# Seven constant products before the first transposes, one weight loaded a place sooner, and x's first two tiles taken singly

## The chip, the cores and the metric

The kernel runs on 1 core of one Trainium2 chip. The metric is the device time of one execution in microseconds (us), inputs and outputs in the chip's memory; lower is better.

## The reference, cut to what matters

For each of 8 graphs with 1024 nodes there are x (1024 x 256) and adj (1024 x 1024, f32, mostly zero). Two layers follow one another; H is the pattern of adj.

```python
H  = (adj != 0);  w = adj[0, :]
Dn = 1 / (H @ w)                    # per node, 0 where the sum is 0
Be = 1 / H.sum(axis=0)              # per column
def conv(x, W, b):
    m = Be[:, None] * (H.T @ (x @ W.T))
    return Dn[:, None] * (H @ m) + b
h  = layer_norm(relu(conv(x, W1, b1)), gamma, beta)
x1 = norm(x + (conv(h, W2, b2) + x))
agg = (adj @ x1) / max(adj.sum(-1), 1e-6)
out = norm(x1 + relu(concat(x1, agg) @ WL.T))
```

## The kernel before

One program works the eight graphs off one after another; `graph(0, ...)` is written out, the others run in a loop. Each engine has its own instruction list, and semaphores tie them together. Nodes are cut into 8 tiles of 128 rows (NT = 8). Every f32 operand of a product with H is split into a high and a low part (`x_hi`, `x_lo`, `m_hi`, `m_lo`), so each product with H is two matmuls.

The stages of a graph on TensorE are S1 (H.T @ x, L1107), S2 (H @ m, transposed, L1183), P and M (times W1: high and low parts, and cross terms, L1211, L1212, L1219), Q (times W2, L1231), S3 and S4 (H.T and H again, L1077), V and VM (times WL) and L (adj @ y, L1077). The next graph's S1 follows.

What concerns the change is the start, up to graph 0's S1. For tile c of adj:

- SyncE's queue (SP) loads the rows, `load_first_rows(c)` (L338), and between them x in pairs of tiles, `load_first_x(j)` (L341), w_row (L357), W1n (L371), W2n (L373) and the rest. SP issues in the order in which these lines stand. ScalarE's own queue loads x's tiles 0 and 1 as one DMA (L527).
- VectorE makes `H[c]` (`build_first_H`, L743), and the low parts of x in pairs (`split_first_x_lo`, L858), then tile c − 2 of the transposed pattern HT (L797), and at some places a row sum of H times w (`sum_Dn`, L758).
- ScalarE makes the high parts of x in pairs (`split_first_x_hi`, L540) and copies the transposed adj out of the banks (`take_adjT`, L571).
- TensorE transposes the tile in two sets of four blocks (`transpose_four`, L1068) and multiplies it into six banks (`s1_step`, L1107), 12 matmuls a tile. In between it transposes the weights: gamma in tile 1, W1 in tile 5, W2 in tile 6, WL in tile 7, each before or between its products, in program order:

```python
for c in range(NT):
    pe.wait_ge(first_rows_loaded[c], 16)
    transpose_adj(c, 0)
    ...
    pe.wait_ge(H_ready, c + 1)
    pe.wait_ge(x_split, c + 1)
    for e in range(N_SIDE):
        if e == 2 and c in BETWEEN:
            transpose_set(BETWEEN[c][0], 0)
        if e == 3 and c > 0:
            transpose_adj(c, 1)
        if e == 5 and len(BETWEEN.get(c, ())) > 1:
            transpose_set(BETWEEN[c][1], 1)
        s1_step(e, c, 0)
```

When six banks are complete, VectorE takes the reciprocals of their column counts (`take_first_rBe`, L840 and L843), ScalarE and VectorE make `m_hi` and `m_lo` (L561, L790), and TensorE works banks 6 and 7. Meanwhile GpSimd adds W2's transposed rows (L441); TensorE's average of them (L1138) uses `mean_n`, a 128 x 128 constant of 1/512. After S1, VectorE does the last row sums, `diagonals` (L890), W1's low and cross parts (L847, L852) and z (L906, L912), GpSimd the cross parts of z (L470), on which M's first product waits.

GpSimd fills the constants first: ident, the ones beside x_hi, eps, zero, mean_n (L417 to L421).

Of the kernel before, what the change touches and what calls it, by code (L numbers as in the profile page):

```python
# [9 lines left out]
ACT = mybir.ActivationFunctionType  # L10

P = 128
# [22 lines left out]
TRANSPOSE_BANKS = (6, 7)  # L35
N_BANKS = 8
Q_FIRST = 5
ROW_BANKS = (0, 1)
ROW_BEHIND = 0
T_SLOTS = 3  # L40
# [8 lines left out]
def graph_net(nc, x, adj, W1, b1, gamma, beta, W2, b2, WL, out):  # L49
    B, C, D = x.shape  # L50
    DH = W1.shape[0]
# [78 lines left out]
    with ctx:  # L130
# [93 lines left out]
        def sem(name):  # L224
            return ctx.enter_context(nc.semaphore(name))
# [4 lines left out]
        raw_loaded = [sem(f"raw_loaded{n}") for n in range(NT // 2)]  # L230
        adjB_loaded = [sem(f"adjB_loaded{n}") for n in range(NT)]
        first_rows_loaded = [sem(f"first_rows_loaded{n}") for n in range(NT)]
        first_x_loaded = [sem(f"first_x_loaded{n}") for n in range(NT // 2)]
        adjT_ready, first_x_hi = (sem(n) for n in ("adjT_ready", "first_x_hi"))
        x_loaded, w_loaded, W2_loaded, W1_loaded, WL_loaded, gamma_loaded, beta_loaded, bias_loaded, table_loaded = (
# [88 lines left out]
        def _(sp):  # L324
# [12 lines left out]
            def load_first_rows(t):  # L337
                sp.dma_start(raw[:, t, :], adj[0, t * P:(t + 1) * P, :]).then_inc(first_rows_loaded[t], 16)  # L338

            def load_first_x(j):  # L340
                sp.dma_start(x_in[:, 2 * j:2 * j + 2, :],  # L341
                             x[0, 2 * j * P:(2 * j + 2) * P, :].rearrange("(t p) d -> p t d", p=P))\
                  .then_inc(first_x_loaded[j], 16)
# [23 lines left out]
            load_first_rows(4)  # L367
            load_first_rows(5)
            load_first_x(3)
            load_first_rows(6)  # L370
            sp.dma_start(W1n[:, :, :], W1.rearrange("(t p) d -> p t d", p=P)).then_inc(W1_loaded, 16)  # L371
            load_first_rows(7)
            sp.dma_start(W2n[:, :, :], W2.rearrange("(t p) d -> p t d", p=P)).then_inc(W2_loaded, 16)  # L373
            sp.dma_start(beta_row[:, :], beta.partition_broadcast(P)).then_inc(beta_loaded, 16)
# [39 lines left out]

        @block.gpsimd
        def _(pool):
            nc.gpsimd.memset(ident[:, :], 0.0).then_inc(ident_zero, 1)  # L417
            nc.gpsimd.memset(x_hi[:, :, D:DP].bitcast(F32), 1.0).then_inc(ones_ready, 1)
            nc.gpsimd.memset(eps_c, NORM_EPS).then_inc(eps_ready, 1)
            nc.gpsimd.memset(zero_c, 0.0).then_inc(zero_ready, 1)  # L420
            nc.gpsimd.memset(mean_n[:, :], 1.0 / DH).then_inc(mean_ready, 1)  # L421
            nc.gpsimd.memset(gW2T[:, :, D:D + 1], 1.0 / DH).then_inc(unit_ready, 1)
            pool.wait_ge(zero_ready, 1)
            pool.wait_ge(ident_zero, 1)
# [99 lines left out]
        @block.scalar  # L524
        def _(act):

            act.dma_start(x_in[:, 0:2, :], x[0, 0:2 * P, :].rearrange("(t p) d -> p t d", p=P))\  # L527
               .then_inc(first_x_loaded[0], 16)
            act.dma_start(gamma_n[0:NH, :], gamma.rearrange("(k p) -> k p", p=P)).then_inc(gamma_loaded, 16)
            act.dma_start(gamma_n[NH:2 * NH, :], b1.rearrange("(k p) -> k p", p=P)).then_inc(gamma_loaded, 16)  # L530
            act.wait_ge(eps_ready, 1)
# [2 lines left out]
            def split_x_hi(b):  # L534
                act.wait_ge(x_loaded, b * IN_B)
                nc.scalar.activation(x_hi[:, :, 0:D], x_in[:, :, :], ACT.Copy).then_inc(x_hi_done, 1)

            def split_first_x_hi(j):
                act.wait_ge(first_x_loaded[j], 16)
                nc.scalar.activation(x_hi[:, 2 * j:2 * j + 2, 0:D], x_in[:, 2 * j:2 * j + 2, :], ACT.Copy)\  # L540
                  .then_inc(first_x_hi, 1)
# [42 lines left out]
                    nc.scalar.activation(gb, set_bank("gamma", 0)[:, 0:2 * NH], ACT.Copy)\  # L584
                      .then_inc(bank_empty[set_of["gamma", 0][0]], 1)

            split_first_x_hi(0)
            for c in range(NT):
                take_adjT(c, 0)
                if c in BETWEEN:  # L590
# [149 lines left out]
        def _(dve):  # L740
# [119 lines left out]

            for c in range(NT):
                build_first_H(c)
                if c % 2 == 0:
                    dve.wait_ge(first_x_hi, c // 2 + 1)
                    split_first_x_lo((c, c + 1))
                if c >= 2:
                    build_HT_columns(c - 2)
                if c in FIRST_DN_AT:
                    sum_Dn(FIRST_DN_AT.index(c), 0, unread, (first_rows_loaded[FIRST_DN_AT.index(c)], 16))
# [188 lines left out]
        def _(pe):  # L1058
            mm = nc.tensor.matmul

            pe.wait_ge(ident_ready, 1)

            def transpose_four(name, part, four):
# [257 lines left out]
```

## Time and profile before

| | |
|---|---|
| median of 3 runs | 1051.92 us (1051.88 to 1051.96) |
| the profiled execution, its own time | 1051.42 us |
| its span | 1049.6 us |
| TensorE, matmuls, busy | 1039.2 us (99%) |
| TensorE, weight loads, busy | 933.2 us (89%) |
| VectorE | 776.7 us (74%) |
| ScalarE | 433.3 us (41%) |
| GpSimd | 435.6 us (41%) |
| memory traffic | 85 GB/s over the span, 353 GB/s from 4.5 to 9.5 us |

The profile is of one execution, and its durations add up to that execution's span. The 1.8 us between its span and its own time lie before and after the instructions. Matmuls are pipelined and their ends are modelled, so the time from the start of one to the start of the next tells the rate. "PEclk" is the clock that the profile says was granted to TensorE, as a share of full speed.

### The profile page before, as it was taken

The numbers are of one execution on the slowest core, as the hardware profiler recorded it, in microseconds if no ns is written. First come the engines' busy times: TensorE is split into PE (matmuls) and PEld (weight loads), VectorE is DVE, ScalarE is ACT, GpSimd is POOL, SyncE is SP. The second block draws the span as 40 slices with busy tenths as digits, with TensorE's granted clock in tenths as the row PEclk, the third lists the DMA queues.
The fourth block names the chain that finished last, engine by engine and source line by source line (L and its number), as shares of the span: only waits on it lengthen the run. The fifth ranks groups of instructions, "written<-read, shape, count | busy, mean of one in ns | idle before, by whom it ended". The sixth has DMA issues, their size and how long they took to land.

```text
span 1049.6 us, 19643 instructions
## 1 busy us (share of the span) xinstructions
PE 1039.2 (99%) x6241; PEld 933.2 (89%) x6241; DVE 776.7 (74%) x1848; ACT 433.3 (41%) x1029; POOL 435.6 (41%) x674
## 2 busy tenths in 40 slices
PE   8999999999999999999999999999999999999997
PEld 8889898898989989899898998989889898888986
DVE  6878786787867878677786778676786777867355
ACT  5553523445234442445325362254622536225350
POOL 0357416434254433534344353543525534265320
PEclk9999999999999999999999999999999999999999
DMA  8065431734227441274414644044440634400001
GB/s 296 3 138 117 98 90 34 152 92 103 64 59 156 96 98 31 60 160 100 90 30 87 133 100 100 20 114 106 100 100 20 142 78 100 110 11 1 2 1 40
DMA packets 72032, 90.01 MB, mean 86 GB/s; under 512 B 15544, under 2 KB 61248, under 8 KB 72000
## 3 DMA queue, kind: packets, MB, share of 16 engines
q1 hardware_dynamic: 63232, 85.49, 35.1%
q10 hardware_dynamic: 8768, 4.10, 1.7%
q8 instruction: 19, 0.31, 0.1%
q14 instruction: 13, 0.11, 0.0%
HBM read 81.14 MB, written 8.42 MB: 85 GB/s over the span
## 4 chain that ended last, share of the span: by engine, by line
PE 99%; DMA 0%; DVE 0%; issue 0%; ACT 0%; DVEq 0%
PE bank L1077 45%; PE bank L1107 12%; PE bank L1183 11%; PE bank L1231 11%; PE bank L1212 3%; PE bank L1219 3%; PE bank L1274 3%; PE bank L1267 3%; PE bank L1268 3%; PE bank L1211 3%; PE bank L1248 1%; PE bank L1068 1%; PE bank L1234 1%; DMA raw<-in_adj_dram 0%; PE bank L1172 0%; DVE xres L779 0%
## 5 line engine op out<-in xcount | busy, mean ns | idle before, releaser
L1077 PE MATMUL bank<-yv,adjT 128*128 128x257 f32 x1024 | 223.3, 379 | 0.0
L1077 PEld LDWEIGHTS bank<-yv,adjT 128*128 128x128 f32 x1024 | 193.6, 189 | 28.7
L566 ACT ACTIVATE small<-mv,small 128x1 f32<-128x1 f32 x192 | 56.0, 291 | 247.8 <-DVE mv L785 144.6
L1077 PE MATMUL bank<-x_hi,H 128*128 128x256 f32 x512 | 125.1, 286 | 0.0
L1231 PE MATMUL bank<-gW2T,hT 128*128 128x257 f32 x512 | 123.7, 385 | 0.0
L1107 PE MATMUL bank<-x_hi,H 128*128 128x258 f32 x512 | 123.6, 289 | 0.0
L1077 PE MATMUL bank<-x_lo,H 128*128 128x256 f32 x512 | 122.4, 280 | 0.0
L1077 PE MATMUL bank<-m_hi,HT 128*128 128x256 f32 x512 | 122.0, 281 | 0.0
L1077 PE MATMUL bank<-m_lo,HT 128*128 128x256 f32 x512 | 121.4, 279 | 0.0
L1107 PE MATMUL bank<-x_lo,H 128*128 128x256 f32 x512 | 119.2, 282 | 0.0
L561 ACT ACTIVATE m_hi<-bank,small 128x256 fp32r<-128x256 f32 x128 | 57.5, 474 | 136.2 <-DVE small L835 75.6
L1231 PEld LDWEIGHTS bank<-gW2T,hT 128*128 128x128 f32 x512 | 93.0, 190 | 11.5
L1183 PE MATMUL bank<-HT,m_lo 128*128 128x512 f32 x256 | 101.8, 398 | 0.0
L1183 PE MATMUL bank<-HT,m_hi 128*128 128x512 f32 x256 | 101.0, 395 | 0.0
L461 POOL TENSOR_TENSOR small<-mv,small 128x1 f32<-128x1 f32 x120 | 30.0, 250 | 170.0 <-DVE small L774 170.0
L1077 PEld LDWEIGHTS bank<-x_hi,H 128*128 128x128 f32 x512 | 96.8, 189 | 0.0
L1077 PEld LDWEIGHTS bank<-x_lo,H 128*128 128x128 f32 x512 | 96.3, 188 | 0.0
L1077 PEld LDWEIGHTS bank<-m_lo,HT 128*128 128x128 f32 x512 | 96.1, 188 | 0.0
L1077 PEld LDWEIGHTS bank<-m_hi,HT 128*128 128x128 f32 x512 | 96.1, 188 | 0.0
L790 DVE SCALAR_TENSOR_TENSOR m_lo<-bank,small,m_hi 128x256 fp32r<-128x256 f32 x128 | 59.2, 481 | 49.3 <-ACT m_hi L561 49.3
L1107 PEld LDWEIGHTS bank<-x_hi,H 128*128 128x128 f32 x512 | 93.9, 190 | 0.5 <-ACT bW_row L607 0.2
L1107 PEld LDWEIGHTS bank<-x_lo,H 128*128 128x128 f32 x512 | 93.1, 190 | 0.2
(132 smaller groups left out, 2203.1 us busy)
## 6 DMA issues: line engine op xcount, KB each, us to landing
raw<-in_adj_dram SPq DMA_DIRECT2D x112, 256.0 KB, 5.8
adjB<-in_adj_dram SPq DMA_DIRECT2D x224, 128.0 KB, 3.1
x_in<-in_x_dram SPq DMA_DIRECT2D x31, 256.0 KB, 6.1
out_dram<-xres SPq DMA_DIRECT2D x108, 64.0 KB, 1.6
raw<-in_adj_dram SPq DMA_DIRECT2D x8, 512.0 KB, 8.8
w_row<-in_adj_dram SPq DMA_DIRECT2D x8, 512.0 KB, 4.7
w_row<-rDn_row ACTq DMA_DIRECT2D x7, 512.0 KB, 9.0
out_dram<-xres SPq DMA_DIRECT2D x4, 256.0 KB, 2.1
```

What stands on the lines that cost most here:

```text
L561: nc.scalar.activation(m_hi[:, e, :], bank(stage, e)[:, 0:D], ACT.Identity, scale=rBe[:, e:e + 1])\
L566: nc.scalar.activation(std[:, i:i + 1], mv[:, which, i, 1:2], ACT.Sqrt, bias=eps_c)\
L790: empties_bank(nc.vector.scalar_tensor_tensor(out=m_lo[:, e, :], in0=bank(stage, e)[:, 0:D], scalar=rBe[:, e:e + 1], in1=m_hi[:, e, :].bit ...
L1077: last = mm(bank(stage, i)[:, 0:n_cols], lhsT, rhs, start=(k == 0 and part == 0), stop=(k == NT - 1 and part == parts - 1))
L1107: last = mm(*args, start=(c == 0 and n == 0), stop=(c == NT - 1 and n == 1))
L1183: last = mm(bank("S2", job)[:, :], m[:, k, d * P:(d + 1) * P], HT[:, k, ch * CH:(ch + 1) * CH], start=(k == 0 and n == 0), stop=(k == NT - ...
L1211: mm(bank("P", j)[:, :], W1_high[:, d, feats], z_high[:, d, nodes], start=(d == 0), stop=False)
L1212: last = mm(bank("P", j)[:, :], W1_low[:, d, feats], z_low[:, d, nodes], start=False, stop=(d == ND - 1))
L1219: last = mm(bank("M", j)[:, :], W1_cross[:, d, feats], z_cross[:, d, nodes], start=(d == 0), stop=(d == ND - 1))
L1231: mm(bank("Q", i)[:, 0:D + 1], hT[:, k, i * P:(i + 1) * P], gW2T[:, k, :], start=(k == 0), stop=(k == NH - 1))
L1267: mm(bank("V", i)[:, :], x1_high[n][:, part], WL_high[:, d, :], start=(d == 0), stop=False)
L1268: last = mm(bank("V", i)[:, :], x1_low[:, n, part], WL_low[:, d, :], start=False, stop=(d == ND - 1))
```

## The change

mean_n is filled first. TensorE, before it waits for ident, multiplies mean_n by itself seven times into bank 7, whose content is not read before it is overwritten. SP issues W1n before adj's tile 6 and no longer behind it. x's tiles 0 and 1 come in two DMAs with a semaphore each, and ScalarE and VectorE split them one at a time: VectorE's list is now H of tile 0, x_lo of tile 0, H of tile 1, x_lo of tile 1.

```diff
+IDLE_PRODUCTS = 7
...
+        first_tiles_loaded = [sem(f"first_tiles_loaded{n}") for n in range(2)]
...
             load_first_x(3)
+            sp.dma_start(W1n[:, :, :], W1.rearrange("(t p) d -> p t d", p=P)).then_inc(W1_loaded, 16)
             load_first_rows(6)
-            sp.dma_start(W1n[:, :, :], W1.rearrange("(t p) d -> p t d", p=P)).then_inc(W1_loaded, 16)
             load_first_rows(7)
...
+            nc.gpsimd.memset(mean_n[:, :], 1.0 / DH).then_inc(mean_ready, 1)
             nc.gpsimd.memset(ident[:, :], 0.0).then_inc(ident_zero, 1)
...
-            nc.gpsimd.memset(mean_n[:, :], 1.0 / DH).then_inc(mean_ready, 1)
...
-            act.dma_start(x_in[:, 0:2, :], x[0, 0:2 * P, :].rearrange("(t p) d -> p t d", p=P))\
-               .then_inc(first_x_loaded[0], 16)
+            for t in range(2):
+                act.dma_start(x_in[:, t, :], x[0, t * P:(t + 1) * P, :]).then_inc(first_tiles_loaded[t], 16)
...
+            def split_first_tile_hi(t):
+                act.wait_ge(first_tiles_loaded[t], 16)
+                nc.scalar.activation(x_hi[:, t, 0:D], x_in[:, t, :], ACT.Copy).then_inc(first_x_hi, 1)
...
-            split_first_x_hi(0)
+            split_first_tile_hi(0)
+            split_first_tile_hi(1)
...
-                if c % 2 == 0:
-                    dve.wait_ge(first_x_hi, c // 2 + 1)
+                if c < 2:
+                    dve.wait_ge(first_x_hi, c + 1)
+                    split_first_x_lo((c,))
+                elif c % 2 == 0:
+                    dve.wait_ge(first_x_hi, c // 2 + 2)
                     split_first_x_lo((c, c + 1))
...
+            pe.wait_ge(mean_ready, 1)
+            for _ in range(IDLE_PRODUCTS):
+                mm(banks[TRANSPOSE_BANKS[1]][:, 0:P], mean_n[:, :], mean_n[:, :], start=True, stop=True)
             pe.wait_ge(ident_ready, 1)
```

TensorE, the start of its list, before (bank is the place of every product; ident and raw are the two operands of a transpose):

```order
L1068 MATMUL bank<-ident,raw 128x128 [waits first_rows_loaded0,ones_ready,ident_ready]
L1068 MATMUL bank<-ident,raw 128x128 x7
L1107 MATMUL bank<-x_hi,H 128x258 [waits bank_empty0,x_split,H_ready]
L1107 MATMUL bank<-x_lo,H 128x256
L1107 MATMUL bank<-x_hi,H 128x258 [waits bank_empty1]
```

TensorE, the same place, now:

```order
L1074 MATMUL bank<-mean_n 128x128 [waits mean_ready]
L1074 MATMUL bank<-mean_n 128x128 x6
L1082 MATMUL bank<-ident,raw 128x128 [waits first_rows_loaded0,ones_ready,ident_ready]
L1082 MATMUL bank<-ident,raw 128x128 x7
L1121 MATMUL bank<-x_hi,H 128x258 [waits bank_empty0,x_split,H_ready]
```

The seven products stand ahead of the first transposes and wait only for mean_n; nothing behind them has changed places.

VectorE, its first tiles, before (H from raw rows, x_lo from x_in and x_hi):

```order
L743 TENSOR_SCALAR H<-raw 128x1024 [waits first_rows_loaded0]
L858 TENSOR_TENSOR x_lo<-x_in,x_hi 128x256 [waits first_x_hi]
L858 TENSOR_TENSOR x_lo<-x_in,x_hi 128x256
L743 TENSOR_SCALAR H<-raw 128x1024 [waits first_rows_loaded1]
L743 TENSOR_SCALAR H<-raw 128x1024 [waits first_rows_loaded2]
```

VectorE, the same place, now (same names):

```order
L750 TENSOR_SCALAR H<-raw 128x1024 [waits first_rows_loaded0]
L865 TENSOR_TENSOR x_lo<-x_in,x_hi 128x256 [waits first_x_hi]
L750 TENSOR_SCALAR H<-raw 128x1024 [waits first_rows_loaded1]
L865 TENSOR_TENSOR x_lo<-x_in,x_hi 128x256 [waits first_x_hi]
L750 TENSOR_SCALAR H<-raw 128x1024 [waits first_rows_loaded2]
```

The second tile's subtraction moved behind H of tile 1; each subtraction waits for its own activation.

## Rows read from the trace of the kernel before

**Rows 1.** The page, chain of waits by engine.

```profile
PE 99%; DMA 0%; DVE 0%; issue 0%; ACT 0%; DVEq 0%
```

**Rows 2.** Timeline of weight loads: start us, us, engine, line, operation [idle before <- releaser].

```profile
4.51 1.57 PEld L1068 LDWEIGHTS bank<-ident,raw 128*128 128x128 f32 x8 [4.51 <-issue]
...
9.49 0.32 PEld L1107 LDWEIGHTS bank<-x_hi,H 128*128 128x128 f32 x1
9.71 0.21 PEld L1107 LDWEIGHTS bank<-x_lo,H 128*128 128x128 f32 x1
9.85 0.19 PEld L1107 LDWEIGHTS bank<-x_hi,H 128*128 128x128 f32 x1
9.97 0.19 PEld L1107 LDWEIGHTS bank<-x_lo,H 128*128 128x128 f32 x1
```

**Rows 3.** Stretch table of PEld: stretch, length, busy (count), granted clock, DMA share, GB/s.

```profile
4.50:9.50 5.00, 4.99 (x25) 1.00 1.05 353
```

**Rows 4.** GpSimd's first fill (timeline), and mean_n's one product (by tile; min/median/max ns).

```profile
0.75 0.20 POOL L417 MEMSET ident<- 128x128 f32 x1 [0.29 <-POOLq L1309]
...
L1138 PE MATMUL bank<-ssum,mean_n x2: 377/377/377, 29.9 to 30.1; 128*128 128x256 f32 x2
```

**Rows 5.** Timeline of ScalarE, the first activation on x.

```profile
4.92 0.63 ACT L540 ACTIVATE x_hi<-x_in 128x512 fp32r<-128x512 f32 x1 [1.23 <-DMA x_in<-in_x_dram]
```

**Rows 6.** Timeline of VectorE: H of tiles 5, 6, 7, HT, reciprocals' start.

```profile
16.77 0.69 DVE L743 TENSOR_SCALAR H<-raw 128x1024 fp32r<-128x1024 f32 x1
...
17.97 0.69 DVE L743 TENSOR_SCALAR H<-raw 128x1024 fp32r<-128x1024 f32 x1
...
20.99 0.69 DVE L743 TENSOR_SCALAR H<-raw 128x1024 fp32r<-128x1024 f32 x1
21.82 0.69 DVE L797 TENSOR_SCALAR HT<-adjT 128x1024 fp32r<-128x1024 f32 x1
...
28.97 0.17 DVE L840 TENSOR_SCALAR small<-bank 128x6 f32<-128x6 f32 x1 [0.75 <-PE bank L1107]
```

**Rows 7.** Timeline of TensorE: first product with tile 5, first transposes of W2.

```profile
19.24 0.37 PE L1107 MATMUL bank<-x_hi,H 128*128 128x258 f32 x1
...
22.99 0.60 PE L1068 MATMUL bank<-ident,W2n 128*128 128x128 f32 x4
```

**Rows 8.** Timeline of SP's queue: issues of adj's tile 6, W1, tile 7, W2.

```profile
5.88 0.47 SPq L338 DMA_DIRECT2D raw<-in_adj_dram  x1
6.39 0.65 SPq L371 DMA_DIRECT2D W1n<-in_L_gnn_W_dram  x1
7.09 3.53 SPq L338 DMA_DIRECT2D raw<-in_adj_dram  x1
10.65 1.07 SPq L373 DMA_DIRECT2D W2n<-in_L_gnn_W_dram  x1
```

**Rows 9.** DMA view, those four: KB, us from issue's start to landing.

```profile
raw<-in_adj_dram SPq DMA_DIRECT2D x1, 512.0 KB, 11.1
W1n<-in_L_gnn_W_dram SPq DMA_DIRECT2D x1, 512.0 KB, 12.1
raw<-in_adj_dram SPq DMA_DIRECT2D x1, 512.0 KB, 12.7
W2n<-in_L_gnn_W_dram SPq DMA_DIRECT2D x1, 512.0 KB, 11.6
```

**Rows 10.** Stretch table: PE, PEld, DVE, ACT, POOL busy (count), clock, DMA share, GB/s.

```profile
30.00:40.00 10.00, 9.96 (x56) 8.38 (x55) 9.41 (x26) 4.82 (x12) 0.00 (x0) 1.00 0.01 2
```

**Rows 11.** Tile raw, first 30 us: row sums, ns min/median/max, first and last start.

```profile
L758 DVE SCALAR_TENSOR_TENSOR unread<-raw,w_row x5: 1218/1220/1470, 15.6 to 26.7; 128x1024 bf16<-128x1024 f32 x5
```

**Rows 12.** Timelines of GpSimd and TensorE: W2's sums, z_cross, first cross product.

```profile
27.21 2.32 POOL L441 TENSOR_TENSOR ssum<-ssum,gW2T 128x256 f32<-128x256 f32 x2
...
49.60 1.29 POOL L470 TENSOR_TENSOR z_cross<-z_high,z_low 128x512 fp32r<-128x512 f32 x1 [0.63 <-DVE z_low L912]
...
51.03 0.71 PE L1219 MATMUL bank<-z_cross,W_cross 128*128 128x512 f32 x2
```

## The prediction

> **What bounds the kernel now.** I read the chain of waits first. It is TensorE for 99% [rows 1], so a change counts only if it moves TensorE's work, all of it, to an earlier time. Then the timeline of TensorE's weight loads: it is idle until 4.51 us, when the first rows of adj are there [rows 2], and from then on its products leave hardly a gap. That hides two things. The first is its rate. The loads start 0.22 us apart at 9.49 and 9.71 us and 0.12 us apart at 9.85 and 9.97, and a load that took 0.32 us takes 0.19 [rows 2]; 258 columns in 0.22 us is the 1.2 GHz level, in 0.12 us about the 2.4 GHz level. The granted clock reads 1.00 in this stretch [rows 3], so that column does not show this step and I go by the spacings. TensorE had been idle until 4.5 us and busy from there to the rise. The second hidden thing is how near its suppliers are: a busy TensorE hides a supplier that comes only just in time. So I take each tile's supplier in turn below.
>
> **The constant products.** mean_n is now the first thing GpSimd fills; such a fill takes 0.20 us and starts at 0.75 [rows 4], so TensorE can start at about 1.0. Each product is a true f32 product, which the trace shows as two MATMULs (one call at L1138, two instructions) [rows 4]: 14 in all. At the low level an instruction of 128 columns takes 1.57/8 = 0.20 us [rows 2], so they last 2.8 to 3.0 us and end near 4.0, before the first transposes at 4.51. They cost nothing as long as the first rows of adj land after 4.0; past that they would cost what they last beyond it. What they can give: if the clock rises once TensorE has been busy from 1.0 on, with only half a microsecond of gap, as long as it was before this rise (5.2 us), it rises at about 6.3 instead of 9.8. The 3.5 us of half-rate work between then takes half as long: **1.75 us** earlier from the second tile on. A rise as early as the first transposes would save another 0.8 us of the 1.57 us there [rows 2], nothing at all is the other end.
>
> **x's first two tiles, singly.** Before, one activation takes both tiles, 0.63 us from 4.92 [rows 5], and VectorE subtracts behind it. Tile 0 alone is half the data and half the activation, so the first subtraction can end some 0.4 us earlier. At the low clock that gives nothing, since the 8 transposes last until 6.08 anyway [rows 2]; with an early rise it supplies TensorE at about 5.6. One more DMA issue on ScalarE's queue (0.5 us) lies ahead of its other work, which leaves it idle until x lands. On VectorE the second tile's subtraction now stands behind H of tile 1; tile 1's products come some 2 us after that. I take 0 for this part.
>
> **Who comes next.** Sum over the suppliers, each as the earliest it lets TensorE be:
> - H of tile 5. It ends at 16.77 + 0.69 = 17.46 [rows 6] and rests on DMA and VectorE's own queue. TensorE's products with tile 5 start at 19.24 [rows 7]. So no gain above 19.24 − 17.46 = **1.8 us** gets past this tile, whatever the clock does.
> - W1 was issued at 6.39 and landed 12.1 us later, at 18.5 [rows 8, 9]; its transposes come after four products with tile 5, so near 19.24 + 0.5 = 19.7, and allow 1.2 us. Put ahead of adj's tile 6 it should land near 17.2, which leaves the way free for 1.8 us.
> - W2, whose place is not changed, was issued at 10.65 and landed 11.6 us later, at 22.25 [rows 8, 9]. Its first transposes started at 22.99 [rows 7]. TensorE takes its work in order, so it stands there: at most **0.7 us** of the gain is left behind this point. About 1 us of new waiting should show here.
> - adj's tile 6 pays for W1. It landed at 5.88 + 11.1 = 17.0 and now should land where W1 did, 18.5 [rows 8, 9]. VectorE started H of tile 6 at 17.97, so this moves by 0.5 us. VectorE then works without a gap, two such operations in 1.20 us (16.77 to 17.97), but waited a little once: 0.83 instead of 0.60 us between 20.99 and 21.82 [rows 6]. That takes up 0.23, so it is 0.3 us late from there. Before the reciprocals for the first six tiles it sat idle for 0.75 us, waiting for TensorE, until 28.97 [rows 6]. It can therefore follow TensorE by 0.75 − 0.3 = **0.45 us** and no more.
>
> Does VectorE's place there matter to TensorE? Yes. From 30 to 40 us VectorE is busy for 9.41 of 10 us [rows 10], all of it one chain, and at its end hang ScalarE's w_row, the z's and GpSimd's z_cross, which ends at 49.60 + 1.29 = 50.89; TensorE's first cross product starts at 51.03 [rows 12]. That is a slack of 0.14 us at most. So TensorE gains what VectorE gains plus about 0.1.
>
> One price inside VectorE is open. Of the five row sums before 28.97 the shortest took 1.218 us, the middle one 1.220 and the last 1.470 [rows 11], which ran while GpSimd added W2's rows, two additions in 2.32 us [rows 12]. With W2's transposes 0.7 us earlier, GpSimd overlaps more of these row sums. Between 0 and 0.25 us more on VectorE; I take 0.1, since only the tail of a second one is met. The Trainium skill, "SBUF — State Buffer", section "SBUF: two separate sides", has a stricter rule: the port pair that VectorE and GpSimd share is an exclusive lock, held for a whole instruction, and the loser blocks fully. By it VectorE could wait for a whole addition more, and the sum below would come out about 0.15 us slower than before instead of 0.45 faster. The row speaks for less: it is 0.25 us longer, not a whole addition.
>
> **The sum.** TensorE could be 1.75 us early by the clock, 1.8 by H, 0.7 by W2; VectorE 0.45 − 0.1 = 0.35, plus 0.1 of slack: 0.45 us. Behind 51 us everything is TensorE's own or follows it, through the loop over the graphs, so this stays to the end. The profiled execution took 1051.42 us, which becomes 1050.97; the median of the runs stands 0.5 above it, at 1051.92, and the forecast is 1051.92 − 0.45 = **1051.5 us**.
>
> **Rivals.**
> - *The clock doesn't rise sooner.* The chip may judge by something other than how long ago the products began. Then TensorE does the same at the same times; VectorE's 0.3 us is covered by its 0.75 us of idle time: 1051.9 us. For it: no row shows what constant operands do to the clock. Against: the three runs lie within 0.08 us, so the rise seems tied to the work. The Trainium skill, "TensorE: Matmul & The Clock Gate", section "What's actually happening", says that the interval the chip judges by runs freely, so the rise moves from run to run. By that rule the gain would vary between none and the full sum. Chance 20%.
> - *The suppliers don't hold.* W2's landing is a figure that no wait in this trace confirms, and if W2 is there a microsecond sooner and tile 6 lands before 18, only H's bound is left: 1.2 to 1.8 us gained, 1050.1 to 1050.7. For it: adj's tile 6 itself landed at 17.0. Chance 15%.
> - *The end is later.* W1's 512 KB ahead of tile 6 delay that tile more than W1's own landing tells. VectorE reaches 28.97 late once H of tile 6 starts after 17.97 + 0.23 + 0.75 = 18.95. If it lands where tile 7 did, 7.09 + 12.7 = 19.8 [rows 8, 9], VectorE is 0.85 late, less 0.1 of slack: 1052.7 us; at 19.2, 1052.1. For it: W1 is read in pieces of a quarter of a row of adj. Against: W1 landed 1.5 us after tile 6, and tile 7 1.3 us after W1, nearly the same for the same bytes. Chance 12%.
> - The forecast's own case, gain between 0.2 and 0.8: 50%. Something else, of either sign: 3%.
>
> **How the numbers follow.** A measurement of this kernel can tell about 0.2%, 2.1 us, from no change. H of tile 5 caps the gain at 1.8 us, and the slower case ends at 0.8 us. So faster by over 0.2% has only what breaks that cap, 4%; slower 2%; within 0.2% 94%. The range runs from the cap, 1050.1, to the middle of the slower case, 1052.2, which leaves out some 10%: what breaks the cap, and the later half of the slower case.
>
> **What would show it.** Right: 14 MATMULs on mean_n from about 1.0 to 4.0 us; weight loads 0.12 us apart from about 6.3; tile 5's products near 17.5; a wait of about 1 us for W2 near 21.3; H of tile 6 at 18.5; the reciprocals' idle time cut to about 0.2 us and started near 28.6; the cross product near 50.6. Wrong: spacings of 0.22 us until 9.7 (first rival); no wait at W2 and a cross product before 50 (second); H of tile 6 after 19 (third); or a saving of more than 2 us, since then a bound that I read as DMA was TensorE's all along.

## The result, and the profile after

| | before | changed |
|---|---|---|
| median | 1051.94 us (8 runs, 1051.71 to 1052.19) | 1055.18 us (8 runs, 1053.71 to 1055.70) |
| ratio | | 1.0030, 95% interval 1.0020 to 1.0039 |
| profiled execution, its own time | 1051.42 us | 1053.71 us |
| its span | 1049.6 us | 1051.9 us |
| TensorE's matmuls busy | 1039.2 us | 1041.5 us |

The change makes the kernel 0.3% slower: 3.2 us by the medians. The forecast of 1051.5 us and its range to 1052.2 are missed. The profiled execution is the fastest of its eight, 1.8 us above the median of before and 2.3 us above the profiled execution of before; the other 1.5 us up to the median of the changed kernel are taken up with the last two experiments. One execution of experiment 5 took 1151.20 us at a mean granted clock of 0.851, and the ratios leave it out. Against the profile of before, TensorE's work is 1.8 us late at 51 us, and 2.3 us at the end. These last 0.5 us come in steps of a few hundredths over the eight graphs; they come with most of the other kernels' profiles as well (−0.1 to 0.6 us, where nothing after 51 us is different), and the profile of before was itself 0.5 us below its median. So I count them as that execution's own and not as the change's.

**The chain of waits is no longer one engine.** Page of the changed kernel, the chain by engine and one group (the last two columns: busy us and mean ns of one; idle before, and what ended it):

```profile
PE 96%; DMA 1%; DVE 1%; SPq 0%; issue 0%; ACT 0%; DVEq 0%; ACTq 0%
...
L1121 PE MATMUL bank<-x_hi,H 128*128 128x258 f32 x512 | 123.2, 288 | 2.3 <-ACT bW_row L614 2.3
```

The share of TensorE fell from 99% [rows 1] to 96%, and in the table the matmuls of this line have a wait of 2.3 us, where they had none. The waits of TensorE in the same profile (us in total, times, longest):

```profile
PE bank L1121 <- ACT bW_row L614: 2.3, 1, 2.3
PE bank L1074 <- POOL mean_n L419: 1.0, 1, 1.0
PE bank L1082 <- ACT adjT L577: 0.5, 1, 0.5
PE bank L1082 <- DMA W2n<-in_L_gnn_W_dram: 0.4, 1, 0.4
```

**TensorE's first microseconds went as intended.** Its weight loads (start us, us, engine, line, operation), which answer to [rows 2]:

```profile
1.01 3.06 PEld L1074 LDWEIGHTS bank<-mean_n 128*128 128x128 f32 x14 [1.01 <-POOL mean_n L419]
4.51 0.90 PEld L1082 LDWEIGHTS bank<-ident,raw 128*128 128x128 f32 x8 [0.45 <-issue]
5.56 0.19 PEld L1121 LDWEIGHTS bank<-x_hi,H 128*128 128x128 f32 x1
5.67 0.19 PEld L1121 LDWEIGHTS bank<-x_lo,H 128*128 128x128 f32 x1
```

Fourteen instructions from 1.01 to 4.07 us, over before the transposes at 4.51, which take 0.90 us instead of 1.57. The first products are 0.11 us apart, so the clock is at its upper level. The record of the granted clock has its rise at 4.66 us, and at 9.74 before. At 9.85 us of the old program TensorE is 1.50 us ahead. At W1 the lead is 1.14 us, behind W2's wait (rows of the timeline of TensorE) still 0.51:

```profile
18.61 0.66 PE L1082 MATMUL bank<-ident,W1n 128*128 128x128 f32 x4 [0.17 <-DMA W1n<-in_L_gnn_W_dram]
...
22.42 0.66 PE L1082 MATMUL bank<-ident,W2n 128*128 128x128 f32 x4 [0.40 <-DMA W2n<-in_L_gnn_W_dram]
...
33.16 0.39 PE L1121 MATMUL bank<-x_hi,H 128*128 128x258 f32 x1 [2.28 <-ACT bW_row L614]
```

At 33.16 us a lead of half a microsecond turns into a delay of 1.73: 2.28 us of idle time in one piece.

**Where that wait comes from.** The chain that ended last, in order of time (start us, us, what), pieces of it from the first 34 us:

```profile
6.49 13.23 DMA raw<-in_adj_dram
...
30.83 0.09 DVE small L847
...
32.10 0.07 ACT m_hi L567
...
32.45 0.38 ACT ssum L613
32.84 0.28 ACT bW_row L614
...
33.16 2.18 PE bank L1121 x16
```

Read it from below: TensorE's next product waits for ScalarE to copy W2's averages out of bank 6 (L613, L614). In ScalarE's list these copies stand behind the first two `m_hi`, which wait for VectorE's reciprocals (L847), which are late because VectorE is, and that goes back without a gap to the landing of adj's tile 6, 13.2 us after its issue. VectorE's timeline, which answers to [rows 6]:

```profile
19.75 0.69 DVE L750 TENSOR_SCALAR H<-raw 128x1024 fp32r<-128x1024 f32 x1 [1.64 <-DMA raw<-in_adj_dram]
...
23.38 0.69 DVE L804 TENSOR_SCALAR HT<-adjT 128x1024 fp32r<-128x1024 f32 x1
...
26.07 1.02 DVE L828 SCALAR_TENSOR_TENSOR unread<-W2n,beta_row 128x512 bf16<-128x512 f32 x1
...
27.02 0.79 DVE L833 COPY bW_wide<-small 128x128 f32<-128x128 f32 x2
27.73 1.76 DVE L765 SCALAR_TENSOR_TENSOR unread<-raw,w_row 128x1024 bf16<-128x1024 f32 x1
...
29.60 1.23 DVE L765 SCALAR_TENSOR_TENSOR unread<-raw,w_row 128x1024 bf16<-128x1024 f32 x1
...
30.75 0.16 DVE L847 TENSOR_SCALAR small<-bank 128x6 f32<-128x6 f32 x1
```

H of tile 6 starts at 19.75 instead of 17.97, 1.78 us late. At 23.38 it is 1.56 (21.82 before): the old wait there took up 0.22. Then the same work takes longer. The second pass over beta takes 1.02 us where the first took 0.69, the two copies take 0.79 (0.36 before, at 25.14 us), and the row sum 1.76 instead of 1.22; the last one is back at 1.23, where before it took 1.47 [rows 11]. That makes 0.33 + 0.43 + 0.54 − 0.24 = 1.06 us more. Without the 0.75 us of idle time that it had, 1.56 + 1.06 − 0.75 = 1.87; the reciprocals are 1.78 late. In just those rows GpSimd adds W2's rows (timeline of GpSimd; the last two additions are one row, and they end at 28.40 us):

```profile
25.91 0.64 POOL L443 TENSOR_TENSOR ssum<-gW2T 128x256 f32<-128x256 f32 x1 [24.16 <-ACT gW2T L560]
26.62 1.78 POOL L443 TENSOR_TENSOR ssum<-ssum,gW2T 128x256 f32<-128x256 f32 x2
```

Before, the first addition and the row sum of 1.47 us (timelines of GpSimd and VectorE):

```profile
26.41 0.72 POOL L441 TENSOR_TENSOR ssum<-gW2T 128x256 f32<-128x256 f32 x1 [24.81 <-ACT gW2T L554]
...
26.75 1.47 DVE L758 SCALAR_TENSOR_TENSOR unread<-raw,w_row 128x1024 bf16<-128x1024 f32 x1
```

A pass of VectorE that starts while an addition runs gets longer by about what is left of that addition. Before, 27.13 − 26.75 = 0.38 us were left and the row sum lost 0.25. In the changed kernel 0.48 us are left when the second pass over beta starts at 26.07, and it loses 0.33; 0.67 are left when the row sum starts at 27.73, and it loses 0.54. The timelines of all fourteen profiles have 22 such passes, and each lost what was left less 0.13 to 0.15 us.

**Where the landing comes from.** DMA view of the changed kernel, W1 (issued at 5.98 us) and adj's tile 6 (issued at 6.49): KB, and us from issue to landing.

```profile
W1n<-in_L_gnn_W_dram SPq DMA_DIRECT2D x1, 512.0 KB, 12.6
...
raw<-in_adj_dram SPq DMA_DIRECT2D x1, 512.0 KB, 13.2
```

W1 lands at 18.6 us and tile 6 at 19.7. W1 is first now, and lands no sooner than when it was second, at 18.5 [rows 8, 9]. Bytes alone don't do that. One more transfer is in the way. The changed kernel's DMA queues from 16.0 to 17.5 us (packets, MB, share of 16 engines):

```profile
q1 hardware_dynamic: 252, 0.57, 103.8%
q8 instruction: 1, 0.02, 4.8%
```

and the kernel before has such a packet only later, from 19.5 to 21.0 us:

```profile
q1 hardware_dynamic: 299, 0.56, 101.0%
q8 instruction: 1, 0.02, 4.6%
```

It is one packet of 16 KB of an engine's instructions (19 of them make 0.31 MB over the kernel). It took 0.048 x 16 x 1.5 = 1.15 us of one of the 16 DMA engines, four times the bytes of a row of adj in one piece. It starts at 19.9 us before and at 16.35 after. If a load is spread over the 16 engines and has landed when the last of them is done, all that is queued behind this packet could land about 1.1 us later. That was my theory when the experiments began, beside the plainer one that W1's bytes are all of it.

### The profile page after: what moved, and what is told of

It reads as the page before. It is cut to its first block, busy times and chain, and to the rows that moved or that the text cites. A ratio compares the mean times of both kernels' runs of the same rounds, so it can differ in the third digit from the quotient of the medians.

```text
span 1051.9 us, 19673 instructions
## 1 busy us (share of the span) xinstructions
PE 1041.5 (99%) x6255; PEld 934.6 (89%) x6255; DVE 778.4 (74%) x1848; ACT 433.2 (41%) x1030; POOL 435.5 (41%) x674
## 4 chain that ended last, share of the span: by engine, by line
PE 96%; DMA 1%; DVE 1%; SPq 0%; issue 0%; ACT 0%; DVEq 0%; ACTq 0%
PE bank L1091 44%; PE bank L1197 11%; PE bank L1245 11%; PE bank L1121 10%; PE bank L1226 3%; PE bank L1233 3%; PE bank L1281 3%; PE bank L1288 3%; PE bank L1225 3%; PE bank L1282 3%; PE bank L1262 1%; DMA raw<-in_adj_dram 1%; PE bank L1248 1%; DVE unread L765 0%; SPq L340 0%
```

## The experiments

Twelve kernels, each with five rounds beside the kernel before; that took 1051.83, 1051.76, 1051.87 and 1051.87 us in the four sets. What the traces show at the places that matter (us; "packet" is the start of the 16 KB instruction packet, "rise" the first rise in the record of the granted clock, the last column TensorE's shift against the profile of before at 51 us):

| kernel | rise | packet | tile 6 lands | W1 lands | H of tile 6 | reciprocals | shift | median us |
|---|---|---|---|---|---|---|---|---|
| before | 9.7 | 19.9 | 17.0 | 18.5 | 17.97 | 28.97 | 0 | 1051.94 |
| changed | 4.7 | 16.4 | 19.7 | 18.6 | 19.75 | 30.75 | +1.8 | 1055.18 |
| W1 back | 4.7 | 17.2 | 17.2 | 19.7 | 18.16 | 29.00 | 0.0 | 1051.91 |
| W1 alone | 7.6 | 19.0 | 18.6 | 17.3 | 18.61 | 28.56 | +0.4 | 1052.22 |
| products alone | 4.8 | 16.2 | 18.5 | 19.7 | 18.44 | 29.02 | +0.2 | 1051.96 |
| no products | 10.7 | 19.9 | 18.4 | 17.1 | 18.42 | 29.42 | +0.5 | 1052.20 |
| tiny products | 7.3 | 15.9 | 18.1 | 19.6 | 18.18 | 28.92 | 0.0 | 1051.89 |
| singles alone | 10.2 | 19.9 | 17.1 | 18.6 | 18.03 | 29.18 | +0.2 | 1051.85 |

**1. The change with W1 behind tile 6 again.**

```diff
             load_first_x(3)
-            sp.dma_start(W1n ...).then_inc(W1_loaded, 16)
             load_first_rows(6)
+            sp.dma_start(W1n ...).then_inc(W1_loaded, 16)
             load_first_rows(7)
```

> The change with W1's load back behind adj's tile 6; everything else of the change stays. Theory A (tile 6, landed 2.7 us later behind W1, holds VectorE, and VectorE holds TensorE): H of tile 6 starts at about 18.0 again, VectorE reaches the reciprocals near 28.2 and waits for TensorE, the 2.3 us wait of TensorE before S1's last bank goes, the span is 1048.5 to 1049.3 and the time about 1051 us. Theory B (the products or the single tiles cost the time): TensorE still waits over 1 us near 31, and the time stays at 1053.5 to 1055.5.

Measured: 1051.91 us (1051.52 to 1052.26), ratio 1.0001, 0.9992 to 1.0010. The loss is gone, and so is the gain. TensorE's waits and VectorE's reciprocals there:

```profile
PE bank L1082 <- DMA W1n<-in_L_gnn_W_dram: 1.3, 1, 1.3
```

```profile
29.00 0.16 DVE L847 TENSOR_SCALAR small<-bank 128x6 f32<-128x6 f32 x1 [0.77 <-PE bank L1121]
```

The lead of 1.5 us that TensorE still has there is spent at W1, 1.3 us of it waiting, and VectorE has its 0.77 us of idle time back. W1 lands at 19.7 though it stands where it stood before, when it landed at 18.5; the packet starts at 17.15 us, when tile 6 is all but there (17.2) and W1 is not.

**2. Before, with W1 sooner and nothing else.**

```diff
+            sp.dma_start(W1n ...).then_inc(W1_loaded, 16)
             load_first_rows(6)
-            sp.dma_start(W1n ...).then_inc(W1_loaded, 16)
```

> The kernel before with W1's load ahead of adj's tile 6 and nothing else. Theory A: H of tile 6 starts at about 19.7, the reciprocals at about 30.5, TensorE waits 1.3 to 2 us before S1's last bank: 1053.3 to 1054 us. Theory B: tile 6's landing costs nothing by itself, 1051.7 to 1052.2 us.

Measured: 1052.22 us (1051.77 to 1052.69), ratio 1.0004, 0.9995 to 1.0013. The theory by which W1's place alone makes the loss falls. VectorE's H of tile 6 in this kernel:

```profile
18.61 0.69 DVE L743 TENSOR_SCALAR H<-raw 128x1024 fp32r<-128x1024 f32 x1 [0.54 <-DMA raw<-in_adj_dram]
```

It lands at 18.6, the 1.5 us later that the forecast had put in, and W1 at 17.3. The clock rose at 7.55 us here, with no constant product. The 0.4 us at 51 us do not come from the wait of the changed kernel: they arise at 30 us, where TensorE waits 0.7 us for GpSimd's sums of W2's rows (L441).

**3. Before, with the products and nothing else.**

```diff
+            pe.wait_ge(mean_ready, 1)
+            for _ in range(IDLE_PRODUCTS):
+                mm(banks[TRANSPOSE_BANKS[1]][:, 0:P], mean_n[:, :], mean_n[:, :], start=True, stop=True)
             pe.wait_ge(ident_ready, 1)
```

> The kernel before with the seven constant products and mean_n filled first, nothing else. Theory A: the clock rises near 4.7 us as in the whole change, tile 6 lands at 17, TensorE waits for W1 (18.5) and W2 (22.3) and comes out 0.4 to 0.7 us ahead: 1051.2 to 1051.5 us. Theory B (products cost): above 1052.5 us.

Measured: 1051.96 us (1051.39 to 1052.57), ratio 1.0002, 0.9993 to 1.0011. SP issues what it issued before, in the same order and within 0.15 us of the same times, yet the loads land later (DMA view: tile 6, issued at 5.96; W1, at 6.53; tile 7, at 7.03):

```profile
raw<-in_adj_dram SPq DMA_DIRECT2D x1, 512.0 KB, 12.5
W1n<-in_L_gnn_W_dram SPq DMA_DIRECT2D x1, 512.0 KB, 13.2
...
raw<-in_adj_dram SPq DMA_DIRECT2D x1, 512.0 KB, 14.0
```

Against 11.1, 12.1 and 12.7 in [rows 9] each takes 1.1 to 1.4 us longer. The packet starts at 16.24 us. TensorE waits 1.2 us for W1, and its lead of 1.4 us is gone.

**4. The changed kernel once more**, with a comment added and nothing else. It also fixes the size of the loss beside the others.

> The changed kernel once more, only a comment added, to see a run of the longer kind (8 runs: one at 1053.7 with a mean granted clock of 0.999, seven from 1055.0 to 1055.7 with 0.997). Theory C (TensorE's 2.3 us of idle time near 31 us makes the clock fall, and some 1.5 us are lost until it rises): the granted clock falls once to half between 31 and 35 us and rises again some us later, and the stages after it start 1.5 us later than in the profile at hand. Rival D: the clock rises later at the start, or falls elsewhere; then the granted clock at 31 to 40 us reads 1.00.

Measured: 1054.52 us (1053.78 to 1055.24, 8 runs), ratio 1.0027, 1.0016 to 1.0038. Four runs took 1053.78 to 1054.11 us with a mean granted clock of 0.998 or 0.999, the other four 1054.93 to 1055.24 with 0.997. The profiled run was again the fastest, with the same 2.3 us of waiting and tile 6 at 19.8, so it shows nothing of theory C, which stays open until experiments 7, 11 and 12.

**5. The change without the products.**

```diff
-IDLE_PRODUCTS = 7
+IDLE_PRODUCTS = 0
```

> The change without its seven products: W1 sooner and x's first tiles singly stay. Theory F (the 16 KB instruction packet of TensorE's own code, which comes sooner when TensorE runs ahead, makes what queues behind it land 1.2 us late): without the products the packet comes at 18 to 19 us, tile 6 lands at 18.6 as with W1's move alone, VectorE reaches the reciprocals near 28.6 and the time is 1052.0 to 1052.5 us. Rival G (the single tiles of x are what costs, by their second DMA or VectorE's order): tile 6 or the reciprocals are late again and the time is above 1053 us.

Measured: 1052.20 us (1051.70 to 1052.37 but for the one execution named above), ratio 1.0003, 0.9994 to 1.0012. Tile 6 lands at 18.4 and W1 at 17.1, the packet is back at 19.86. VectorE's timeline:

```profile
18.42 0.69 DVE L750 TENSOR_SCALAR H<-raw 128x1024 fp32r<-128x1024 f32 x1 [0.48 <-DMA raw<-in_adj_dram]
...
29.42 0.17 DVE L847 TENSOR_SCALAR small<-bank 128x6 f32<-128x6 f32 x1 [0.76 <-PE bank L1121]
```

Half a microsecond late at tile 6, and 0.76 us of slack left at the reciprocals: covered, as the prediction's first rival had it. The 0.5 us in the column of shifts come from a rise at 10.65 us in this execution. Why the median of the runs stands 0.4 us above before is not shown by it.

Experiments 1, 2, 3 and 5 show an effect of the two parts together. Either part alone costs 0.4 us or less by the medians, which lies within the intervals; each delays tile 6, by 1.4 to 1.6 us (W1 ahead of it) and by 1.1 to 1.5 us (the products, or the tiny ones of experiment 8), and 17.0 + 1.5 + 1.2 = 19.7 is where it lands when both are there. The prediction's deciding point, 18.95 us, is 1.95 us behind the old landing: room for one of them and not for two.

**6. The change with one row sum moved behind the reciprocals.**

```diff
-            for t in (3, 4):
-                sum_Dn(t, 0, unread, (first_rows_loaded[t], 16))
+            sum_Dn(3, 0, unread, (first_rows_loaded[3], 16))
             take_first_rBe()
+            sum_Dn(4, 0, unread, (first_rows_loaded[4], 16))
```

> The change with VectorE's row sum of tile 4 moved from ahead of the reciprocals to behind them. Theory V (TensorE's wait near 31 us is VectorE's lateness): the reciprocals start 1.2 us sooner, at 29.5, TensorE waits 1.1 us instead of 2.3, and since some 0.6 us of VectorE's own idle time behind the reciprocals is filled, the end comes 0.5 to 0.7 us sooner: 1053.1 us, and in no run does the mean granted clock read 0.997. Rival: something else than VectorE holds S1's last bank, TensorE still waits over 2 us and the time stays at 1053.7 or above.

Measured: 1052.42 us (1051.84 to 1052.76, 11 runs), ratio 1.0005, 0.9996 to 1.0014. Tile 6 is as late as in the change (H at 19.73), but the reciprocals start at 29.39 and TensorE's wait shrinks (waits of TensorE):

```profile
PE bank L1121 <- ACT bW_row L614: 0.5, 1, 0.5
```

With 1.2 us less ahead of the reciprocals 2.0 of the 2.7 us of experiment 4 are gone, more than expected. So most of the loss, whatever lies upstream, passes through this place. The 0.7 us that remain lie within the interval; in the profile TensorE is 0.15 us late until 50 us and 0.5 from the first cross product on. No run had a clock of 0.997, which already hinted at where the rest went.

**7. The change with two spare passes on VectorE ahead of the reciprocals** (what they compute is not used).

```diff
+            for n in range(2):
+                ...
+                nc.vector.scalar_tensor_tensor(out=unread[:, :], in0=raw[:, 3, :], scalar=0.0, in1=w_row[:, :],
+                                               op0=ALU.not_equal, op1=ALU.mult).then_inc(spare, 1)
             for t in (3, 4):
```

> The change with two more passes of a row sum's kind (1.2 us each, results unused) ahead of the last two row sums before the reciprocals. Theory V: everything from the reciprocals on comes 2.4 to 2.7 us later, the time is 1056.2 to 1058 us, and TensorE's wait near 31 us is 4.7 us or more. Theory C (idle time of TensorE there makes its clock fall): the granted clock falls once to half near 31 to 35 us, in the profile too, and the time is 1.3 us more. Rival D: no fall in the granted clock.

Measured: 1057.23 us (1056.50 to 1057.79), ratio 1.0050, 1.0037 to 1.0064. TensorE waits 4.4 us, a little less than the 4.7 of Theory V, and starts again 3.7 us late; at 34.4 us of the old program it is 5.9 us late. The extra is in the stretch table (stretch, length, busy with counts of PE, PEld, DVE, ACT, POOL, granted clock, DMA share, GB/s):

```profile
33.40:34.60 1.20, 0.00 (x0) 0.00 (x0) 0.60 (x3) 0.92 (x3) 0.00 (x0) 0.50 0.00 0
34.70:38.00 3.30, 2.88 (x13) 2.88 (x14) 3.30 (x8) 2.87 (x8) 0.00 (x0) 0.50 0.00 0
```

The granted clock falls to 0.50, the 1.2 GHz level, at 33.33 us while TensorE is idle, and stays there for 6.8 us.

**8. Before, with sixteen products of a single column** (32 short matmuls, not used).

```diff
+            pe.wait_ge(mean_ready, 1)
+            for _ in range(16):
+                mm(banks[TRANSPOSE_BANKS[1]][0:1, 0:1], mean_n[:, 0:1], mean_n[:, 0:1], start=True, stop=True)
             pe.wait_ge(ident_ready, 1)
```

> The kernel before with sixteen products of one column by one column (32 short matmuls) in TensorE's first 4 us; its own work keeps its place and, as I expect, its late clock rise. Theory F: they move TensorE's code forward by 32 pairs, so the 16 KB instruction packet comes at 15.5 to 17.5 us instead of 19.9, and tile 6, W1 or tile 7, whichever queue behind it, land about 1.2 us later than before (17.0, 18.5, 19.8), with the same DMA issues and TensorE no faster. Rival: they land late only where TensorE runs faster (contention for the memory), so here they land at 17.0, 18.5 and 19.8. Time 1051.6 to 1052.4 us either way.

Measured: 1051.89 us (1051.61 to 1052.39), ratio 1.0001, 0.9992 to 1.0011. They add 32 matmuls, with their weight loads, and hardly any work. The packet starts at 15.90 us, and tile 6 (issued at 5.92 us) and W1 (6.49) land late again (DMA view):

```profile
raw<-in_adj_dram SPq DMA_DIRECT2D x1, 512.0 KB, 12.2
...
W1n<-in_L_gnn_W_dram SPq DMA_DIRECT2D x1, 512.0 KB, 13.1
```

One condition of this experiment was not met: the clock rose at 7.28 us, and TensorE was 1.17 us ahead at 9.85 us. So it does not exclude the rival by itself. Experiment 9, below, does. There TensorE is as far ahead (1.09 us) without any product, the packet starts at 18.99 us, and tile 6 (issued at 5.78 us) and W1 (6.42) land at 17.2 and 18.6, no more than 0.2 us later than before (DMA view of experiment 9):

```profile
raw<-in_adj_dram SPq DMA_DIRECT2D x1, 512.0 KB, 11.4
...
W1n<-in_L_gnn_W_dram SPq DMA_DIRECT2D x1, 512.0 KB, 12.2
```

In experiment 7, where W1 is ahead of tile 6 as in the changed kernel, the packet starts at 16.61 us and not at 16.35. There W1, issued at 5.79 us, lands at 17.4 instead of 18.6, and tile 6 behind it is late as ever, at 19.6 (DMA view of experiment 7):

```profile
W1n<-in_L_gnn_W_dram SPq DMA_DIRECT2D x1, 512.0 KB, 11.6
```

So the landings go with the place of the packet: a load behind it is late and a load ahead of it is not. That the packet is TensorE's is inferred: at nearly the same lead it comes 3.1 us sooner where TensorE has 64 more instructions (15.90 against 18.99), and with the same instructions 0.9 us sooner where TensorE is 1.1 us ahead (18.99 against 19.88); the view does not name its engine.

**9. Before, with the two spare passes.** The reciprocals alone come late; loads, products and everything before them are as they were.

> The kernel before, with two spare passes of 1.22 us on VectorE ahead of the last two row sums, so that only the reciprocals come later, by 2.44 less the 0.75 us of idle time: near 30.7 us, as in the changed kernel, but with every load and TensorE's own start as before. The passes compute nothing that is used. If a late VectorE is all that the change costs, TensorE waits about 1.7 us there and the kernel takes 1053.5 us, each of its runs within 0.3 of that. If idle time of this size is also paid for with a lower granted clock later, runs with a clock of 0.997 appear and the median is 1054.5 to 1055.2, as for the changed kernel. If the change costs through something else than this wait (its loads, or what the products leave behind), then 1053.5 with a clock of 0.998 in every run.

Measured: 1053.99 us (1053.70 to 1054.37, 11 runs), ratio 1.0020, 1.0011 to 1.0029. The waits of TensorE, and the start of the reciprocals in VectorE's timeline:

```profile
PE bank L1147 <- POOL ssum L442: 1.2, 1, 1.2
PE bank L1116 <- ACT bW_row L608: 1.1, 1, 1.1
```

```profile
31.45 0.15 DVE L841 TENSOR_SCALAR small<-bank 128x6 f32<-128x6 f32 x1
```

They start at 31.45 and not at 30.7, since four passes in a row met GpSimd's additions and took 1.4 to 1.6 us each; TensorE is 2.05 us late at 51 us. 1051.87 + 2.05 = 1053.9: the waits account for the time, and no run had a clock below 0.998. So a late VectorE is enough to make a loss of this size. The second reading, the one with the lower clock, falls here: idle time of 1.2 and 1.1 us, in two pieces, was not followed by a lower clock.

**10. Before, with x's first two tiles singly and nothing else** (the part of the change's diff on `first_tiles_loaded`, unchanged).

> The kernel before, with x's first two tiles loaded and taken apart singly, and no other part of the change. My theory: nothing, 1051.8 us within 0.3; H of tile 6 starts at 18.0, the reciprocals at 29.0, tile 6 lands near 17.0. Its rival, that the second issue on ScalarE's queue and the later activations share in the loss: x's second tile lands 1 us or more after the first, H of tile 6 starts after 18.3, and the time is above 1052.3.

Measured: 1051.85 us (1051.63 to 1052.45, 11 runs), ratio 1.0001, 0.9992 to 1.0010; tile 6 at 17.1, the reciprocals at 29.18. No time is lost, as forecast, but the first sign of the rival is there. Tile 1's half (ScalarE's timeline, 4.92 for both tiles in [rows 5]) comes much later:

```profile
6.56 0.42 ACT L541 ACTIVATE x_hi<-x_in 128x256 fp32r<-128x256 f32 x1 [1.49 <-DMA x_in<-in_x_dram]
```

In the changed kernel's profile this activation starts at 6.71 us, holds ScalarE's copy of adjT until 7.03 and so gives TensorE its 0.5 us wait. In experiment 4, the same program, it starts at 6.36 us and TensorE does not wait.

**11. The change with one spare pass** (experiment 7 with `range(1)`).

> The changed kernel with one spare pass of 1.22 us (its result is not used) on VectorE ahead of the reciprocals, half of what the two passes added. The idle time of TensorE there becomes 2.3 + 1.2 = 3.5 us in one piece. If only the wait counts, the time is that of the changed kernel's fastest runs, 1053.8, plus 1.2 to 1.5: 1055.1 in nearly all runs. If the long idle time is also followed by a fall of the granted clock in some runs (as it was by one of 6.8 us in the run with 4.4 us idle), the profiled run or most of the others show a clock of 0.996 to 0.997 and take 1056 to 1057, and in the profile, if it is one of these, the fall begins 1 to 5 us after the idle time.

Measured: 1056.06 us (1055.94 to 1056.52), ratio 1.0041, 1.0027 to 1.0054. TensorE waits 3.1 us, and all five runs have a clock of 0.997. In the profile it falls at 34.43 us for 3.4 us, 0.4 us after the idle time and not 1 to 5; at 51 us the shift is 4.1 us.

**12. The change without the singles**: products and W1's place together.

> The changed kernel with x's first two tiles loaded and taken apart as one again, so products and W1 sooner alone. My theory: these two together are the whole loss: tile 6 lands at 19.7, H of tile 6 starts after 19.5, TensorE waits about 2.3 us for the row of bank 6, 1053.8 to 1055.2 us. Its rival, that the singles carry a part (their kernel alone takes nothing, but here they would come on top): H of tile 6 at 19.2 or before, a wait below 1.5 us and 1053.0 or less.

Measured: 1054.89 us (1053.75 to 1055.98, 7 runs), ratio 1.0026, 1.0015 to 1.0037. These two parts are the whole loss: H of tile 6 at 19.96, and this wait of TensorE:

```profile
PE bank L1111 <- ACT bW_row L608: 2.3, 1, 2.3
```

And its profiled run, at 1055.34 us, is in the longer of two groups of times. The stretch from 34.7 to 38.0 us in this kernel (columns as in experiment 7):

```profile
34.70:38.00 3.30, 3.30 (x13) 2.93 (x12) 3.27 (x9) 1.52 (x4) 0.00 (x0) 0.50 0.00 0
```

and in the changed kernel's profile, of 1053.71 us:

```profile
34.70:38.00 3.30, 3.30 (x19) 2.75 (x18) 3.27 (x9) 1.39 (x3) 0.00 (x0) 1.00 0.00 0
```

With the same wait, the clock is at half for 3.4 us from 34.63 on in the one and not in the other, and TensorE does 13 matmuls instead of 19. Its shift is 1.9 us before this stretch and 3.5 behind it. That is the missing part of the median. Over the whole run 3.4 us at half lower the mean granted clock by 3.4 x 0.5 / 1053 = 0.0016, about the step from 0.999 to 0.997 in the runs' records. Over this kernel and the two sets of the change there are 23 runs: 8 took 1053.71 to 1054.11 us, 15 took 1054.89 to 1055.98, and none lies between. The two profiles in the shorter group have no fall; the one in the longer group has it.

## Why the prediction was wrong

**The step that failed** is "adj's tile 6 pays for W1. It landed at 5.88 + 11.1 = 17.0 and now should land where W1 did, 18.5". It landed at 19.7. The exchange of W1 and tile 6 was right by itself (18.4 to 18.6 in experiments 2 and 5). What I left out is that the products change the landings too: they move TensorE's instruction packet from 19.9 to about 16.3 us, ahead of tile 6's last rows, for 1.2 us (experiments 3 and 8). I had treated the loads' landing times as given, and costed the parts of the change one at a time. Behind this step two more terms failed: the contention on VectorE, put at 0.1 us, came to 1.06, and a clock that falls after idle time, for which the sum had no term, cost 1.2 to 1.5 us in most runs.

Point by point:

- *Constant products, at no cost of their own:* right. 14 MATMULs from 1.01 to 4.07 us.
- *Rise at about 6.3 instead of 9.8, 1.75 us:* right in sign, and the size is in part luck. The rise came at 4.66 and the lead at 9.85 us was 1.50 us, after the 0.5 us wait for adjT. In the seven other profiles with these products it was 1.15 to 1.91 us, with rises between 3.91 and 7.12 us: the rise is no fixed time, below.
- *W1 near 17.2:* it landed at 18.6, again the packet's 1.2 us and more; 17.1 and 17.3 without products.
- *W2 leaves at most 0.7 us:* right. The wait is there (0.40 us), and 0.51 us of lead were left behind it.
- *Port contention, 0.1 us:* far too small. It was 1.06 us, because VectorE was late by 1.6 us and met all of GpSimd's additions with operations that it had met with one before. I had moved GpSimd's additions against a VectorE in its old place. I had also misread the row: it was 0.25 us longer and "not a whole addition" because it had started when only 0.38 us of an addition were left. The Trainium skill, "SBUF — State Buffer", section "SBUF: two separate sides", calls the shared port pair an exclusive lock held for a whole instruction. The rows agree with it: each of the 22 passes lost what was left of the addition that was running, less 0.13 to 0.15 us.
- *VectorE may follow by 0.45 us:* it fell back by 1.78.
- *Behind 51 us nothing more:* right (+1.79 there).

**The rival "The end is later" is the one that happened**, to which I gave 12%. Its mechanism, its deciding point (H of tile 6 after 18.95) and even its landing, 19.8, were right; its reason, the bytes of W1, was half of it. Its price was 1052.7. By its terms VectorE would be 0.85 us late; with contention it was 1.78. TensorE's delay of 1.73 us gives 1051.9 + 1.7 = 1053.6, near the shorter group of runs, 1053.7 to 1054.1. The 1.2 to 1.5 us above them, which make the median, are a term that I did not have at all: a clock that falls again after idle time. Of the rival *"The clock doesn't rise sooner"* only this holds, that the rise moves from run to run; it did come sooner. *"The suppliers don't hold"* is refuted: TensorE waited for W2, and tile 6 did not land before 18.

So 3.2 us = 1.7 (tile 6 late through two causes, contention included) + 1.2 to 1.5 (the fall of the clock, in two thirds of the runs), with the rest within what one execution differs from another.

No version here beats the kernel before. The best with the products (1, 3) are its equal: their 1.5 us is taken back at W1, which lands at 19.7. Whether W1's transposes could be put a tile later, so that the gain gets past it, was not tried; from the lead left behind W2 I estimate 0.5 us at most.

## What to carry to other kernels

Cost the parts of a change together where they feed the same consumer: here two delays of one landing, 1.5 and 1.2 us, each fitted into 1.95 us of slack, and their sum did not. Here an instruction load moved when TensorE got ahead or got more instructions, and it shares the DMA engines with the data; in a stretch where these are full, look where these packets lie before taking a landing time as given. And the price of an idle piece of TensorE is not only its length: look through the runs for two groups of times, and profile one of the longer group.

## What the runs showed of the hardware

- **One 16 KB instruction packet delayed tile 6, W1 and tile 7 by 1.1 to 1.5 us each where they were queued behind it**, and not where they were ahead of it (experiments 1, 3, 7, 8 and 9), with the DMA engines full (104% and 101% busy in the stretches above). It lies at 19.9 us in the three kernels without products whose clock rose late (before, 5 and 10), at 19.0 where it rose at 7.4 or 7.6 us (9 and 2), and at 15.9 to 17.2 where TensorE had more instructions.
- **VectorE's passes and GpSimd's additions excluded each other.** A pass that started during an addition lost 0.25, 0.33 or 0.54 us where 0.38, 0.48 or 0.67 us of the addition were left. The other way round, the first addition took 1.69 us in experiment 2, where it started at 25.85 just behind a row sum (25.83), and 0.64 us in the changed kernel.
- **The rise of the clock is not at a fixed time.** With TensorE idle until 4.5 us in each, it came at 9.74, 7.55, 10.65, 7.42 and 10.18 us in the profiles of before and of experiments 2, 5, 9 and 10; with the seven products between 3.91 and 7.12 (seven profiles and the changed kernel's). The products bring it about 4 us forward on the mean, and either group spreads over 3.2 us. I had argued that three times within 0.08 us tie it to the work. They were too few: thirty runs of the kernel before, beside experiments 1 to 4, lie from 1051.39 to 1052.23 us, and what a sooner rise gains is taken back by suppliers later on. The Trainium skill, "TensorE: Matmul & The Clock Gate", section "What's actually happening", says that the interval by which the chip judges runs freely; the spread of these rows agrees.
- **The clock falls again after idle time in the middle of a kernel**, to half, for 3.4 or 6.8 us. By times and mean clocks it did in 15 of 23 runs with one idle piece of 2.3 us, in all ten with one of 3.1 or 4.4 us, and in none of eleven with two pieces of 1.2 and 1.1 us. The fall of 3.4 us cost 1.5 us more than the idle time (experiments 11 and 12), the one of 6.8 us 2.2 us (experiment 7). It was seen itself in three profiles (7, 11, 12); for the other runs it is inferred from times and mean clocks.
- **Taking a DMA in two halves made the second much later**: x's tile 1 was worked from 4.9 us as part of one DMA, and from 6.3 to 6.8 as one of its own behind tile 0, while tile 0 was worked from 4.6 to 4.7 (eight profiles). Why is open.
